# A second place table's products moved into the first expert's up product, in a decoder layer on one Trainium2 core

## The reference

```python
logits = where(old_to_new == -1, -inf, x @ gate_weight.T)      # 128 experts, 48 of them kept
top_v, top_i = top_k(softmax(logits), 8);  top_v /= sum(top_v)
pos = place of the token among those that chose the same expert, in token order
xb[e, pos] = x[token]            for pos < CAP = 192
g, u = split(xb[e] @ gate_up_proj[e].T, 2)                     # 2 x 192
out[e] = (silu(g) * u) @ down_proj[e].T
final[token] += top_v * out[e, pos]
```

## Time and profile before

| | us |
|---|---|
| runs, median (lowest to highest) of 3 | 932.47 (931.37 to 936.32) |
| profiled execution, its own time | 932.39 |
| its span, first to last instruction | 930.6 |
| busy PE / DVE / POOL / ACT | 832.6 / 634.5 / 466.5 / 400.2 |
| mean granted TensorE clock | 0.963 |

### The profile page before, as it was taken

One profiled execution on the slowest core, in us unless ns is written; L12 is line 12 of the kernel. 1 busy time (PEld: TensorE's weight loads), 2 busy tenths in 40 slices (PEclk: granted clock), 3 DMA queues, 4 the chain that ended last, 5 costly groups with the idle time before them and its releaser, 6 DMA issues. The chain is left out here.

```text
span 930.6 us, 18478 instructions
## 1 busy us (share of the span) xinstructions
PE 832.6 (89%) x5918; PEld 707.0 (76%) x5919; DVE 634.5 (68%) x1446; ACT 400.2 (43%) x820; POOL 466.5 (50%) x441
## 2 busy tenths in 40 slices
PE   6799999999999989999999689999999999999600
PEld 4577777777777778888888588998998998898500
DVE  6755776567765765777777886778676776776425
ACT  4323323333333322223222156666666666666404
POOL 0233233433234231556555547787777777776344
PEclk9999999999999999999999899999999999999955
DMA  9542111211111016232222399999999999998675
GB/s 337 183 183 69 47 47 45 90 45 45 45 64 61 25 54 231 74 109 97 89 102 87 117 267 295 288 287 291 285 287 295 291 291 293 296 251 191 147 197 198
DMA packets 72798, 155.75 MB, mean 167 GB/s; under 512 B 9953, under 2 KB 10609, under 8 KB 72369
## 3 DMA queue, kind: packets, MB, share of 16 engines
q1 hardware_dynamic: 50240, 99.81, 33.3%
q0 software_dynamic: 22512, 55.37, 23.9%
HBM read 110.29 MB, written 44.86 MB: 167 GB/s over the span
## 5 line engine op out<-in xcount | busy, mean ns | idle before, releaser
L1975 POOL DMA_INDIRECT y_rows<-arena,place_token x96 | 157.1, 1636 | 80.9 <-issue 54.7
L1964 POOL DMA_INDIRECT xg<-x_rows,place_token x96 | 95.7, 997 | 36.6 <-issue 27.4
L988 PE MATMUL ps<-arena,raw 128*128 128x192 f32 x576 | 99.7, 331 | 2.8 <-DVE arena L1782 2.8
L988 PEld LDWEIGHTS ps<-arena,raw 128*128 128x128 f32 x576 | 95.9, 193 | 5.5 <-issue 3.7
L607 PE MATMUL ps<-w_hi,x_hi 128*128 128x512 f32 (+1 forms) x332 | 79.0, 361 | 10.3 <-ACT arena L1025 4.7
L1837 POOL TENSOR_TENSOR arena<-arena,attn_pack 128x512 f32<-128x512 f32 x12 | 16.0, 1337 | 121.9 <-DVE arena L1343 121.9
L607 PE MATMUL ps<-w_hi,x_lo 128*128 128x512 f32 (+1 forms) x332 | 74.9, 348 | 0.0
L607 PE MATMUL ps<-w_lo,x_hi 128*128 128x512 f32 (+1 forms) x332 | 74.1, 346 | 0.0
L988 PE MATMUL ps<-arena,mid_flat 128*128 128x192 f32 x432 | 73.1, 326 | 0.0
L988 PEld LDWEIGHTS ps<-arena,mid_flat 128*128 128x128 f32 x432 | 70.7, 190 | 1.5
L607 PEld LDWEIGHTS ps<-w_hi,x_hi 128*128 128x128 f32 x332 | 53.6, 194 | 22.8 <-issue 9.5
(11 more groups left out here) (242 smaller groups left out, 1958.9 us busy)
## 6 DMA issues: line engine op xcount, KB each, us to landing
raw<-in_gu SPq DMA_DIRECT2D x24, 768.0 KB
mid_flat<-in_gu SPq DMA_DIRECT2D x18, 768.0 KB
raw<-in_dn SPq DMA_DIRECT2D x24, 256.0 KB
y_rows<-zero SPq DMA_DIRECT2D x20, 256.0 KB
mid_flat<-in_dn SPq DMA_DIRECT2D x18, 256.0 KB
arena<-in_gu SPq DMA_DIRECT2D x6, 768.0 KB
arena<-in_xT SPq DMA_DIRECT2D x16, 256.0 KB, 3.3
x_res<-in_x SPq DMA_DIRECT2D x16, 256.0 KB, 2.7
```

Source lines behind the costliest of these rows:

```text
L988: m = pe.matmul(out, wgu[slot][:, q, part * P:(part + 1) * P], xgT[:, p, q, :], start=(q == 0), stop=(q == KC - 1))
L1964: pool.indirect_dma_start(out=xg[:, place, h, :], out_offset=None, in_=x2_d, in_offset=bass.IndirectOffsetOnAxis(ap=place_token[:, 2 * n + ...
L1975: pool.indirect_dma_start(out=y2_d if p and n < DUAL else y_d, out_offset=bass.IndirectOffsetOnAxis(ap=place_token[:, 2 * n + h:2 * n + h ...
```

## The change

For experts 2 to 7 the one-hots are made later on DVE: `hot_b` behind the scan of `so_far(second)`, `hot_a` and `hot_id` behind `copy_x(0)` and `keep_w(0)`. On PE `ahead_of(second)` stands directly behind `keep_warm` 6, and `c_turn(0)` follows; the second table's 16 products stand inside `c_up(0)` between its second and third part, its spreading product behind the third. DVE masks it inside expert 0's step behind line 1776 and cuts it behind `copy_x(1)`. So `place_made` 2, for which the gather of expert 2 waits, is raised inside expert 0's step. `places(second)` is split over the places ahead of experts 1 and 2, and PE waits for its first instruction (`tstep` 11) ahead of `c_down(0)`. In the loop every table step is two experts later: PE at `m` = 2 and 3, DVE mask at 2, cut at 3, `one_hots_b` at 4 and 5, `one_hots_a` at 0 and `hot_ids` at 1; for the first full group, `one_hots_b` is ahead of and behind expert 2. GpSimd takes the gather of 8, 16, ... in turn n = 6, 14, ... instead of one turn earlier.

```diff
--- before.py
+++ after.py
@@ -945,9 +945,9 @@
             def between(g, m):
                 if isinstance(g, int):
                     return
-                if m == 0:
+                if m == 2:
                     table(g + 2)
-                if m == 1:
+                if m == 3:
                     spread_table(g + 2)
 
             first, second = slice(0, GE), slice(GE, E2)
@@ -957,11 +957,9 @@
             table(0, 0, FIRST)
             spread_table(0, FIRST)
             flags_by_token(1, 1)
-            keep_warm(BH, 4)
-            table(1, FIRST, GE - FIRST)
+            keep_warm(BH, 6)
+            ahead_of(second, BY + 1, 2)
             keep_warm(BH, 2)
-            spread_table(1, GE - FIRST)
-            ahead_of(second, BY + 1, 2)
             pe.wait_ge(tstep, 5)
 
 
@@ -977,7 +975,7 @@
                         m = pe.transpose(ps[:, CT + q // 2, o:o + HALF], xg[:, place, h, q * P:(q + 1) * P], eye[0:HALF, 0:HALF])
                 m.then_inc(c_turned[p], 1)
 
-            def c_up(p, k, slot, turn):
+            def c_up(p, k, slot, turn, after=None):
 
                 pe.wait_ge(*weights_of(slot, turn))
                 pe.wait_ge(c_copied, 2 * (2 * k + p + 1))
@@ -986,7 +984,10 @@
                     out = ps[:, CG, part * CAP:(part + 1) * CAP] if part < 2 else ps[:, CG + 1, 0:CAP]
                     for q in range(KC):
                         m = pe.matmul(out, wgu[slot][:, q, part * P:(part + 1) * P], xgT[:, p, q, :], start=(q == 0), stop=(q == KC - 1))
-                m.then_inc(gu_made[p], 1)
+                    if part == 2:
+                        m.then_inc(gu_made[p], 1)
+                    if after:
+                        after(part)
 
             def c_down(p, k):
                 pe.wait_ge(dn_split[p], k + 1)
@@ -1003,11 +1004,19 @@
 
             def c_expert(n, p, k, left, slot, turn):
                 first, last = is_first(n), left == 0
-                c_up(p, k, slot, turn)
+                c_up(p, k, slot, turn, rest_of_group if first else None)
                 if not last:
                     c_turn(1 - p, k + p, *next_place(slot, turn))
+                if isinstance(n, int) and n == 1:
+                    pe.wait_ge(tstep, 11)
                 if not first:
                     c_down(1 - p, k - (1 - p))
+
+            def rest_of_group(part):
+                if part == 1:
+                    table(1, FIRST, GE - FIRST)
+                if part == 2:
+                    spread_table(1, GE - FIRST)
 
             c_turn(0, 0, 0, 0)
             keep_warm(CG + 1, 2)
@@ -1665,20 +1674,22 @@
                                        sel_t[:, ns, :].rearrange("p n j -> p (n j)"), 0.0, ALU.mult, ALU.add).then_inc(tab_v, 1)
                 dve.wait_ge(tab_v, done + 2)
 
-            def places(ns, bank, done):
+            def places(ns, bank, done, parts=(0, 1)):
 
                 size = ns.stop - ns.start
-                dve.wait_ge(pos_made, 1 if bank == 0 else 2)
-                dve.tensor_tensor(count[:, ns, :], sel_so_far[:, ns, :], ps[:, bank, ns].unsqueeze(2).to_broadcast([P, size, NT]), ALU.add).then_inc(tstep, 1)
-                dve.wait_ge(tstep, done + 1)
-                dve.scalar_tensor_tensor(place_i[:, ns, :], count[:, ns, :], float(NBB - 1), sel_t[:, ns, :], ALU.add, ALU.mult).then_inc(tstep, 1)
-                dve.wait_ge(tstep, done + 2)
-                dve.tensor_single_scalar(a_i[:, ns, :], place_i[:, ns, :], 4, ALU.arith_shift_right).then_inc(tstep, 1)
-                dve.tensor_single_scalar(b_i[:, ns, :], place_i[:, ns, :], NBB - 1, ALU.bitwise_and).then_inc(tstep, 1)
-                dve.wait_ge(tstep, done + 4)
-                dve.tensor_copy(a_h[:, ns, :], a_i[:, ns, :]).then_inc(tstep, 1)
-                dve.tensor_copy(b_h[:, ns, :], b_i[:, ns, :]).then_inc(tstep, 1)
-                dve.wait_ge(tstep, done + 6)
+                if 0 in parts:
+                    dve.wait_ge(pos_made, 1 if bank == 0 else 2)
+                    dve.tensor_tensor(count[:, ns, :], sel_so_far[:, ns, :], ps[:, bank, ns].unsqueeze(2).to_broadcast([P, size, NT]), ALU.add).then_inc(tstep, 1)
+                    dve.wait_ge(tstep, done + 1)
+                    dve.scalar_tensor_tensor(place_i[:, ns, :], count[:, ns, :], float(NBB - 1), sel_t[:, ns, :], ALU.add, ALU.mult).then_inc(tstep, 1)
+                if 1 in parts:
+                    dve.wait_ge(tstep, done + 2)
+                    dve.tensor_single_scalar(a_i[:, ns, :], place_i[:, ns, :], 4, ALU.arith_shift_right).then_inc(tstep, 1)
+                    dve.tensor_single_scalar(b_i[:, ns, :], place_i[:, ns, :], NBB - 1, ALU.bitwise_and).then_inc(tstep, 1)
+                    dve.wait_ge(tstep, done + 4)
+                    dve.tensor_copy(a_h[:, ns, :], a_i[:, ns, :]).then_inc(tstep, 1)
+                    dve.tensor_copy(b_h[:, ns, :], b_i[:, ns, :]).then_inc(tstep, 1)
+                    dve.wait_ge(tstep, done + 6)
 
             def part_of(z, g, n0, size):
                 return z[:, bass.ds(g * GE + n0, size), :].rearrange("p n j -> p j n")
@@ -1705,28 +1716,26 @@
 
             def between(g, m):
                 if isinstance(g, int):
-                    if m == 5:
+                    if m == 6:
+                        places(second, BY + 1, 10, (0,))
+                    if m == 7:
+                        places(second, BY + 1, 10, (1,))
                         dve.wait_ge(tab_made, 2)
                         one_hots_b(1, halves=(0,))
-                    if m == 6:
-                        one_hots_b(1, halves=(1,))
-                        one_hots_a(1)
-                    if m == 7:
-                        hot_ids(2)
                     return
                 if m == 0:
+                    one_hots_a(g + 1)
+                if m == 1:
+                    hot_ids(g + 2)
+                if m == 2:
                     mask_table(g + 2)
-                if m == 1:
+                if m == 3:
                     cut_table(g + 2, (g + 1) * GE)
-                if m == 2:
+                if m == 4:
                     dve.wait_ge(tab_made, g + 3)
                     one_hots_b(g + 2, halves=(0,))
-                if m == 3:
+                if m == 5:
                     one_hots_b(g + 2, halves=(1,))
-                if m == 4:
-                    one_hots_a(g + 2)
-                if m == 7:
-                    hot_ids(g + 3)
 
             first, second = slice(0, GE), slice(GE, E2)
             dve.wait_ge(flags_in, 16)
@@ -1736,16 +1745,11 @@
             one_hots_b(0, 0, FIRST)
             one_hots_a(0, 0, FIRST)
             hot_ids(0, 0, FIRST)
-            one_hots_b(0, FIRST, GE - FIRST, (0,))
+            spread_flags(BY_PE - 1, (SLOT_T - 1) % 4, 1).then_inc(flagged, 1)
             mask_table(0, FIRST)
             cut_table(0, 0, FIRST)
-            spread_flags(BY_PE - 1, (SLOT_T - 1) % 4, 1).then_inc(flagged, 1)
-            one_hots_b(0, FIRST, GE - FIRST, (1,))
-            one_hots_a(0, FIRST, GE - FIRST)
-            hot_ids(1, FIRST, GE - FIRST)
             so_far(second, 2)
-            mask_table(1, GE - FIRST)
-            cut_table(1, FIRST, GE - FIRST)
+            one_hots_b(0, FIRST, GE - FIRST)
 
             CT, CG, CY = 0, 2, 4
             LO, HI = slice(0, P // 2), slice(P // 2, P)
@@ -1775,6 +1779,8 @@
                 dve.tensor_tensor(wdn_lo[p][:, 0, :], wdn[slot], wdn_hi[p][:, 0, :].bitcast(F32), ALU.subtract)
                 dve.tensor_tensor(wdn_lo[p][LO, 1, :], wdn_rest[slot], wdn_hi[p][rest_rows[slot], 1, :].bitcast(F32), ALU.subtract)\
                    .then_inc(dn_split[p], 1)
+                if first:
+                    mask_table(1, GE - FIRST)
                 dve.wait_ge(g_made, 2 * (2 * k + p) + 1)
                 at_least(dve, dn_made[p], k)
                 dve.tensor_tensor(h_a[:, p, :], ps[:, CG, CAP:2 * CAP], g_a[:, :], ALU.mult).then_inc(h_made, 1)
@@ -1782,6 +1788,8 @@
                 dve.tensor_tensor(h_c[HI, p, :], ps[HI, CG + 1, 0:CAP], g_c[HI, :], ALU.mult).then_inc(h_made, 1)
                 if not last:
                     copy_x(1 - p, k + p)
+                if first:
+                    cut_table(1, FIRST, GE - FIRST)
                 dve.wait_ge(h_high, 2 * k + p + 1)
                 dve.tensor_tensor(ha_lo[:, p, :], h_a[:, p, :], ha_hi[:, p, :].bitcast(F32), ALU.subtract)
                 dve.tensor_tensor(hc[HI, p, :], h_c[HI, p, :], hc_hi[HI, p, :].bitcast(F32), ALU.subtract).then_inc(h_split, 1)
@@ -1789,10 +1797,13 @@
                     scale_y(1 - p, k - (1 - p))
                 if not last:
                     keep_w(n + 1, 1 - p, k + p, (slot + 1) % 4)
+                if isinstance(n, int) and n == 2:
+                    one_hots_b(1, halves=(1,))
 
             copy_x(0, 0)
             keep_w(0, 0, 0, 0)
-            places(second, BY + 1, 10)
+            one_hots_a(0, FIRST, GE - FIRST)
+            hot_ids(1, FIRST, GE - FIRST)
```

(7 more changed lines are left out.)

## The result

The changed kernel takes 962.57 us (median of 4 runs, 955.76 to 966.34); the kernel before, beside it, 934.39. The ratio is 1.030, with a 95% interval of 1.026 to 1.034: **28 us slower**. I had forecast 934.5, no change that could be told.

What follows compares the result with a forecast made beforehand. PE's work was taken to bound steady work, with transfers saturated too and gains only at the start. Terms -0.5 + 1.6 + 1.1 = +2.2 us on 932.39 gave 934.6, stated as 934.5 us; range 930.7 to 938.5.

Steps and rivals of the forecast that it cites:

- The first list's rows: Start: the first gather issue is no longer held by a DVE one-hot; expert 0's turn comes 2.1 us earlier (0.7 to 2.9).
- Expert 1's up product: Start: it begins 2.7 us earlier, at 541.2, and at full clock takes 4.0 us instead of 5.8.
- Half clock behind the wait for expert 2: Expert 2's turn: PE idles 3.8 us and then pays half of 3.3 us at half clock, +1.6 us.
- DVE's load in experts 2 and 3: Start: extra DVE work ahead of experts 2 and 3 makes PE idle, +1.1 us (0 to 2).
- the lower bound of a gather's landing: Gathered rows: a steady gather's 0.39 MB had moved about 2.4 us behind its issue.
- the group edges: Loop: the gather of 8, 16, ... one turn later still lands in time, costed at nothing.
- its cover: Turns of 8, 16, ...: data need to about 591.8, the turn is at 591.95; spare time only some 0.5 us.
- rival 2: Turns of 8, 16, ... to 40: the gather lands late; each 0.7 us costs 3.5 in all, 938 us; chance 0.12.
- The issue's end: Loop: the moved gather's issue ends where that of expert 9 ended, at 589.34, or 0.4 us earlier.
- its sign: Loop: waits at every eighth turn would show the prediction wrong.
- expert 2: Start: its rows land 3.9 us behind the issue, so its turn starts at 549.0 against 549.53, 0.5 us gained.
- the middle: Expert 2's rows: landing taken as 3.9 us behind the issue, between rows of 2.4 and 5.3 us.

Runs made afterwards that it cites:

- e6: Kernel before with only GpSimd's gather of 8, 16, ... moved behind the scatter, tables early as before; 957.99 us against 930.14, ratio 1.033.
- e1: Changed kernel with GpSimd's gather of 8, 16, ... ahead of the scatter, tables still late; 937.13 us against 924.97 of the kernel before, ratio 1.011.
- e8: Kernel before with loop table steps one expert later, GpSimd's order kept, one-hots of experts 8 to 15 moved on from expert 0; 924.05 us against 926.31, ratio 0.998.
- e2: Changed kernel with the weights of experts 4 to 7 loaded only once expert 2's rows have landed; ratio 1.028 to the kernel before.
- e3: Kernel before with table steps two experts later and the gather behind the scatter, start kept except later one-hots of experts 8 to 15; 945.31 us against 924.97, ratio 1.020.
- e7: Changed kernel with 11 units of TensorE filler between expert 1's up product and expert 2's turn; 963.78 us against 963.50 of the changed kernel.
- e4: Changed kernel with the gather ahead of the scatter and weights of experts 4 to 7 behind expert 2's rows; 932.29 us against 924.97 of the kernel before, ratio 1.008.

## Why the prediction was wrong

**What held.** The first list's rows: the first issue fell from 2.75 us to 0.94, as DVE ran no one-hot beside it, and the turn came 1.8 us earlier (forecast 2.1). The issue at 533.70, which did have a one-hot beside it, took 1.61 us and ended 0.8 us behind it. The Trainium skill's statement on two SBUF inputs ("SBUF — State Buffer", Practical consequences) fits this again, and its inference on `tensor_tensor` does not. Expert 1's up product began 2.8 us earlier (forecast 2.7) and ran at full clock. Half clock behind the wait for expert 2 cost 1.5 us (forecast 1.6): from turn to up product it was 4.50 us, against 2.98. DVE's load in experts 2 and 3 cost 0.9 us (forecast 1.1), with one PE wait of 0.4 us for the copy. These terms were right to 0.3 us.

**The step that failed** is one reading: the lower bound of a gather's landing, "the 0.39 MB of a steady gather, issued by 589.34, had moved by 591.8, about 2.4 us behind the earlier trace rows". Those bytes were not the gather's. The trace of before could have told it. There 0.39 MB in 205 packets are 1.9 KB a packet; the gathers of experts 0 and 1, alone in the queue between 530 and 534 us, moved 0.46 MB in 135 packets, 3.4 KB each. The next stretch of the kernel before, 592 to 594.2 us, is the gather of expert 9:

```profile
q0 software_dynamic: 135, 0.43, 63.5%
```

That is 3.2 KB a packet, ending 4.9 us behind the issue. What moved from 589 to 592 was a scatter: 192 rows of 2,048 bytes are 0.39 MB. The single records of the trace say it outright: the data packets of gathers have 4,480 bytes, those of scatters 2,048, and the first of 4,480 bytes for expert 9 starts at 591.97. The same signature is in the changed kernel, from 598 to 600 us (2.2 KB a packet: mostly scatter) and from 600 to 603 (3.2 KB: gathers):

```profile
q0 software_dynamic: 102, 0.22, 53.4%
```

```profile
q0 software_dynamic: 266, 0.85, 99.5%
```

The rows of expert 8, issued by 597.51, move in the second stretch, and the turn starts at 602.78.

**What followed from it.** First, the group edges. The prediction costed them at nothing, with "its cover is only some 0.5 us", and put the point from which rival 2 decides at "a landing more than 2.9 us behind the issue". The issue's end was placed rightly (7.8 to 8.1 us behind the up product of expert 6; forecast 8.1 or 0.4 less), but the landing is 5.3 to 7.2 us. Rival 2 was the case, with 2.4 to 4.3 us beyond the point, and its sign, waits at every eighth turn, is what the profile shows. Its price was short too: it counted only the lateness, 0.7 us per 0.7, and left out the half clock that follows. Waits of 16.8 us in all cost 26.7 at the edges. I had priced this clock loss at expert 2, and not at the five edges. Second, expert 2: I took 3.9 us as the middle between 2.4 and 5.3; it was 7.5, above both ends, and the wait was 7.5 us instead of 3.8. So the turn came 3.2 us later than before instead of 0.5 earlier.

A second weakness was the middle itself. The 5.3 us of the earlier trace rows came from the very situation in question, rows fetched beside a queue full of weights. That row should have been the value, and by it alone the edges would have had waits of 2.4 us each.

**What settles the cause.** e6 puts 29.3 us of edge cost on GpSimd's order alone; e1 takes it from 26.7 to 6.3 by the order alone, and e8, with an earlier list, has none. e2 shows that at expert 2 the landing is long because of the weights in front: 2.3 us without them, 7.5 with them. No run took the weights away at an edge. So that they make the landing long there too, and how much of it the scatter in front takes, is argued and not shown. Open is also why the landing at the edges varies between 5.3 and 8.2 us (the longest at expert 40 in e2).

## What to carry to other kernels

The kernel before issued these rows nine microseconds ahead of their use, and five to eight of the nine were needed: before an issue is moved, find its landing time under the load that it will meet, and tell the transfers of one queue apart by bytes per packet before reading a landing from it. Waits of 2 to 4.4 us on TensorE cost another 1.7 to 2.8 us each in half clock at the edges of the changed kernel, so waits that recur in a loop are priced with it. And operations of 1 to 3 us ahead of a short chain can be worth more than they seem: moving the one-hots of experts 8 to 15 one place on shortened the first seven steps by 2.7 us in e8, since the wait ahead of expert 1's up product fell from 2.8 to 1.6 us and the half clock behind it went.

## What the runs showed of the hardware that I had not expected

Rows that GpSimd had issued by 546.65 and 548.14 us got nothing from the DMA engines until 550.3, while SP's queue ran, but for two instruction packets, alone and at full rate (DMA view of the changed kernel, 546.7 to 550.2 us: packets, MB, share):

```profile
q1 hardware_dynamic: 614, 1.15, 102.5%
```

The same came again in e1, where the second half of expert 8's rows, issued by 585.95, had its first bytes at 589.2 (587.2 to 589.1 us; GpSimd's queue had one small packet in it):

```profile
q1 hardware_dynamic: 350, 0.69, 102.7%
```

Once served, the two queues shared the engines about evenly in the changed kernel: from 550.2 to 553 us GpSimd's had 46.7% and SP's 59.4% of their time. The Trainium skill, "DMA: Bandwidth & Descriptors" (Queues, rings and completion order), says that each engine alternates between the queues that have work, a packet of several descriptors at a time. The even sharing agrees; that rule alone would not give 3.5 us without a byte, and no run here shows what holds them.

The landing behind the end of an issue was much the same with a scatter issued directly ahead (5.3 to 8.2 us over the edges of the changed kernel, e2, e3, e6 and e7) and without (5.8 to 7.3 in e1 and e4). With the scatter its bytes filled a part of that time, as in e6; without it the queue stood still for a part of it, as in e1. Why the two come out alike is open.
